# Expert tiles of 512 and of 256 slots, filled by a placement in units of 256, in place of 23 tiles of 512

## The reference

```python
gout = x @ Wgate + bgate
topv, topi = jax.lax.top_k(gout, K)              # K = 2 of E = 8
topw = jax.nn.softmax(topv, axis=-1)
...
z = (x @ W1[e] + b1[e]) * (x @ W2[e] + b2[e])     # 128 -> 256
g = z @ Wg[e] + bg[e]                             # 256 -> 256
o = g * sigmoid(g) * (z @ Wl[e] + bl[e])
y = o @ W3[e] + b3[e]                             # 256 -> 128
```

## Time and profile before

| what | value |
|---|---|
| median of 3 runs | 958.55 us (958.43 to 963.51) |
| profiled execution: span from the first to the last instruction | 882.4 us |
| median less that span: what lies around it | 76.15 us |
| PE / DVE / POOL / ACT busy, share of the span | 75% / 64% / 52% / 34% |
| mean granted TensorE clock | 0.842 of full |
| instructions | 31011 |

### The profile page before, as it was taken

The page is one execution under the profiler, slowest core; times in us unless marked ns, Lnnn a source line. Parts: engine busy times, 40 slices in busy tenths (PEclk is TensorE's granted clock), DMA queues, the critical chain, the costliest instruction groups (busy, mean ns, idle before and its releaser), DMA issues.

```text
span 882.4 us, 31011 instructions
## 1 busy us (share of the span) xinstructions
PE 658.0 (75%) x13276; PEld 502.2 (57%) x13276; DVE 568.8 (64%) x1233; ACT 299.6 (34%) x519; POOL 458.6 (52%) x519
## 2 busy tenths in 40 slices
PE   2434856877687878878898686978878788899772
PEld 2223845666465656566666555666566646676651
DVE  6888957536747865965577546864477748533573
ACT  2221024323343425342254334333433343334230
POOL 3730168634826754676475755387435662723323
PEclk9985567989887968997899898898889798999775
DMA  7221121323113214131332204131324311310350
GB/s 290 107 96 54 61 54 39 105 64 86 26 39 78 64 32 114 39 77 53 88 108 64 77 14 108 44 92 38 54 61 74 69 38 45 93 53 31 107 196 12
DMA packets 62488, 64.92 MB, mean 74 GB/s; under 512 B 39824, under 2 KB 47888, under 8 KB 62224
## 3 DMA queue, kind: packets, MB, share of 16 engines
q1 hardware_dynamic: 54880, 46.84, 17.8%
q0 software_dynamic: 5888, 12.07, 6.1%
q10 hardware_dynamic: 1584, 4.04, 1.2%
HBM read 45.35 MB, written 17.56 MB: 71 GB/s over the span
## 4 chain that ended last, share of the span: by engine, by line
PE 29%; issue 21%; POOL 20%; DVE 18%; DMA 6%; ACT 3%; SPq 3%; DVEq 0%; POOLq 0%; ACTq 0%
PE ps_shared L1629 5%; PE ps_shared L1850 4%; POOL y_d L1042 4%; POOL xs L1031 3%; PE ps_g L1625 3%; PE ps_l L1625 3%; PE ps_x L1625 3%; DVE acc L1392 3%; PE ps_shared L1767 3%; POOL sumsq L996 2%; SPq L881 2%; DMA system_d<-masked 2%; DVE solve_prod L1466 2%; PE ps_shared L1625 2%; POOL ssq_o L1068 2%
## 5 line engine op out<-in xcount | busy, mean ns | idle before, releaser
L1042 POOL DMA_INDIRECT y_d<-work,put_i x92 | 92.3, 1004 | 80.5 <-DVE work L1605 57.4
L1031 POOL DMA_INDIRECT xs<-xn_d,owner_i x92 | 94.7, 1030 | 60.2 <-issue 24.6
L1625 PE MATMUL ps_x<-xr,w_up 128*128 128x512 f32 x276 | 98.4, 476 | 17.9 <-issue 12.0
L1076 POOL TENSOR_TENSOR z<-work,z 128x512 fp32r<-128x512 f32 x46 | 60.4, 1314 | 59.5 <-ACT z L1246 59.3
L1625 PE MATMUL ps_g<-z,w_mid 128*128 128x512 f32 x276 | 83.2, 441 | 4.6 <-POOL z L1076 4.2
L1625 PE MATMUL ps_l<-z,w_mid 128*128 128x512 f32 x276 | 82.2, 436 | 1.7 <-issue 1.1
L1392 DVE SCALAR_TENSOR_TENSOR acc<-pre,late_sb,acc 128x512 f32<-128x512 f32 x72 | 59.9, 832 | 26.9 <-ACT acc L1139 25.6
L1625 PEld LDWEIGHTS ps_x<-xr,w_up 128*128 128x128 f32 x276 | 54.8, 218 | 36.5 <-issue 18.9
L1850 PE MATMUL ps_shared<-w_plain,work 128*128 128x128 f32 x368 | 58.2, 323 | 18.1 <-DVE work L1600 13.3
L1466 DVE TENSOR_TENSOR solve_prod<-solve_T,solve_L 128x1 f32<-128x1 f32 (+14 forms) x120 | 49.4, 412 | 28.7 <-DMA solve_L<-system_d 25.3
L1850 PEld LDWEIGHTS ps_shared<-w_plain,work 128*128 128x128 f32 x368 | 53.9, 232 | 22.6 <-issue 16.5
(11 more groups left out here) (252 smaller groups left out, 1420.7 us busy)
## 6 DMA issues: line engine op xcount, KB each, us to landing
w_split<-expert_split SPq DMA_DIRECT2D x23, 768.0 KB
w_plain<-expert_plain SPq DMA_DIRECT2D x23, 196.0 KB
xa_d<-xr SPq DMA_DIRECT2D x8, 512.0 KB, 2.6
xa<-xa_d SPq DMA_DIRECT2D x8, 512.0 KB, 4.0
system_d<-masked SPq DMA_DIRECT2D x8, 256.0 KB, 2.9
x_res<-hidden SPq DMA_DIRECT2D x8, 256.0 KB, 2.8
xs<-xn_d,owner_i POOLq DMA_INDIRECT x92
y_d<-work,put_i POOLq DMA_INDIRECT x92
```

The costliest lines, as they stand in the source:

```text
L1031: pool.indirect_dma_start(xs[par][:, c, :], None, xn_d.rearrange("w p (c d) -> (w p c) d", c=CPW), bass.IndirectOffsetOnAxis(owner_i[:, w ...
L1042: pool.indirect_dma_start(y_d, bass.IndirectOffsetOnAxis(put_i[:, w * CPW + c:w * CPW + c + 1], 0), y_sb[par][:, c * D:(c + 1) * D], None) ...
L1076: pool.tensor_tensor(low[:, :], up1[i], high[:, :].bitcast(FP), ALU.subtract).then_inc(S["z_low"], 1)
L1625: made = pe.matmul(to, weights[a], x[b], start=start and n == 0, stop=stop and n == 2)
```

## The change

The number of slots goes from 23 * 512 = 11776 to 16 * 512 + 7 * 256 = 9984. `UNITS = (8192 + 8 * 255) // 256 = 39` units of 256 slots, two to a big tile and one to a small one. Tiles 0 to 15 are big, tiles 16 to 22 are small. All steps of a small tile work on half the columns, with 2 gathers and 2 scatters in place of 4 and 4. Its weights are loaded and split as before. `place` now counts, for each expert, pairs of units and an odd unit, gives the pairs to big tiles and the odd ones to small tiles (pairs beyond the 16 big tiles go on into small ones), and numbers slots so that 128 neighbours share a column. `flow` gets estimates for the small tiles; `PULL` and `LEAN` stay.

```diff
-TILES = (2 * SEQS * STEPS + EXPERTS * (TILE - 1)) // TILE
-SLOTS = TILES * TILE
+UNIT = TILE // 2
+UNITS = (2 * SEQS * STEPS + EXPERTS * (UNIT - 1)) // UNIT
+BIG = 2 * SEQS * STEPS // TILE
+TILES = BIG + UNITS - 2 * BIG
-LANES = TILES * CPW
+LANES = UNITS * CPW // 2
+SLOTS = LANES * P
...
+def columns(t):
+    return CPW if t < BIG else CPW // 2
+def width(t):
+    return columns(t) * P
...
+    if name == "split" and w >= WINDOWS + BIG:
+        return [[(ACT_, 0.4)], [(DVE_, 0.45)]]
...
+    if name in FLOW_SMALL and w >= BIG:
+        return FLOW_SMALL[name]
...
+FLOW_SMALL = {
+    "load_xs": [[(POOL_, 2.6, 5.1)]],
+    "up1": [[(PE_, 0.6)], [(ACT_, 0.5)]], "up2": [[(PE_, 0.6)]], "z": [[(DVE_, 0.45)], [(ACT_, 0.45)]], "zlow": [[(POOL_, 0.75)]],
+    "mid_g": [[(PE_, 1.2)], [(ACT_, 0.5)]], "mid_l": [[(PE_, 1.2)]], "swish": [[(DVE_, 0.45)]], "times": [[(DVE_, 0.45)]],
+    "down": [[(PE_, 1.2)]], "y_out": [[(DVE_, 0.45)]], "y_put": [[(POOL_, 2.6, 5.5)]],
+}
...
-                    for c in range(CPW):
+                    for c in range(columns(w)):
+                        lane = lane_at(w) + c
                         pool.indirect_dma_start(xs[par][:, c, :], None, xn_d.rearrange("w p (c d) -> (w p c) d", c=CPW),
-                                                bass.IndirectOffsetOnAxis(owner_i[:, w * CPW + c:w * CPW + c + 1], 0)).then_inc(
+                                                bass.IndirectOffsetOnAxis(owner_i[:, lane:lane + 1], 0)).then_inc(
                                                     S[f"in_xs{par}"], 16)
...
-                    follow(dve.tensor_reduce(tiles_of[:, :], over512[:, :, :], AX.X, ALU.add))
-                    follow(dve.tensor_tensor_scan(tiles_upto[:, :], ones8[:, :], tiles_of[:, :], 0.0, ALU.mult, ALU.add))
...
+                    dve.tensor_reduce(odd_of, reached[:, :, 0], AX.X, ALU.add)
+                    follow(dve.tensor_reduce(pairs_of, reached[:, :, 1], AX.X, ALU.add))
+                    follow(dve.tensor_tensor(odd_of, odd_of, pairs_of, ALU.subtract))
+                    dve.tensor_tensor_scan(pairs_upto, ones8[:, :], pairs_of, 0.0, ALU.mult, ALU.add)
+                    follow(dve.tensor_tensor_scan(odd_upto, ones8[:, :], odd_of, 0.0, ALU.mult, ALU.add))
+                    follow(dve.tensor_scalar(all_odd[:, :], odd_upto[:, EXPERTS - 1:], EXPERTS - 0.5, None, ALU.is_gt))
...
+                    follow(dve.scalar_tensor_tensor(extra, over(pairs_of.unsqueeze(2), *by_expert), float(TILE), upto[:, :, :],
+                                                    ALU.mult, ALU.is_le))
+                    dve.scalar_tensor_tensor(extra, over(shift_of[:, :].unsqueeze(2), *by_expert), float(UNIT), extra,
+                                             ALU.mult, ALU.mult)
...
-                    for whole, of, size in ((quad_f, slot_f, CPW), (tile_f, quad_f, P)):
-                        follow(dve.tensor_scalar(whole, of[:, :, :], 1.0 / size, 0.5 / size - 0.5, ALU.mult, ALU.add))
-                        follow(dve.tensor_scalar(whole, whole, ROUND, None, ALU.add))
-                        follow(dve.tensor_scalar(whole, whole, -ROUND, None, ALU.add))
...
+                    follow(dve.tensor_scalar(column_f[:, :, :], slot_f[:, :, :], 1.0 / P, 0.5 / P - 0.5, ALU.mult, ALU.add))
+                    follow(dve.tensor_scalar(column_f[:, :, :], column_f[:, :, :], ROUND, None, ALU.add))
+                    follow(dve.tensor_scalar(column_f[:, :, :], column_f[:, :, :], -ROUND, None, ALU.add))
...
-                    product(ps_x1[:, :], [up_of(w, part, 0, i) for part in range(2)], x).then_inc(S["x1"], 1)
+                    product(ps_x1[:, 0:width(w)], [up_of(w, part, 0, i) for part in range(2)], x).then_inc(S["x1"], 1)
...
-                    for c in range(CPW):
+                    for c in range(columns(w)):
                         for k in range(FJ):
                             made = pe.matmul(ps[:, c * D:(c + 1) * D], gated[par][k][:, c * P:(c + 1) * P], down_of(w, k),
                                              start=k == 0, stop=k == FJ - 1)
```

More of the change, by code:

```diff
@@ L45, with lane_at, rows_moved @@
 FLOOR_MIN, FLOOR_MAX = 0.01, 0.1
+def columns(t):
+    return CPW if t < BIG else CPW // 2
+def width(t):
+    return columns(t) * P
+def lane_at(t):
+    return sum(columns(n) for n in range(t))
+def rows_moved(t):
+    return 16 * sum(columns(n) for n in range(t % 2, t + 1, 2))
 class Seq:
@@ new lines, in _ @@
+                    dve.tensor_scalar(units_of[:, 0:2, EXPERTS - 1], units_of[:, 0:2, EXPERTS - 1], all_odd[:, :], None, ALU.subtract)
+                    follow(dve.tensor_scalar(units_of[:, 2:4, EXPERTS - 1], units_of[:, 2:4, EXPERTS - 1], all_odd[:, :], None, ALU.add))
+                    dve.tensor_tensor(base_of[:, :], pairs_upto, pairs_of, ALU.subtract)
+                    follow(dve.tensor_scalar(last_of[:, 0], pairs_upto, 2.0, -2.0 * BIG, ALU.mult, ALU.add))
+                    follow(dve.tensor_scalar(beyond[:, :], last_of[:, 0, EXPERTS - 1:], 0.0, None, ALU.max))
@@ L1338, in _ @@
+                    follow(dve.tensor_scalar(last_of[:, 1], odd_upto, beyond[:, :], None, ALU.add))
+                    dve.tensor_tensor(past[:, :, :], over(tile_at[:, :].unsqueeze(2), P, TILES, 2 * EXPERTS),
+                                      over(last_of[:].rearrange("p q e -> p (q e)").unsqueeze(1), P, TILES, 2 * EXPERTS), ALU.is_ge)
+                    follow(dve.tensor_tensor(shift_of[:, :], last_of[:, 1], odd_of, ALU.subtract))
                     dve.tensor_reduce(row_f[:, :], past[:, :, :], AX.X, ALU.add)
+                    follow(dve.tensor_tensor(shift_of[:, :], shift_of[:, :], last_of[:, 0], ALU.subtract))
@@ L1344, in _ @@
                                                     upto[:, :, :], ALU.mult, ALU.add))
+                    follow(dve.tensor_tensor(upto[:, :, :], upto[:, :, :], extra, ALU.add))
                     for k, mine in enumerate((top1, top2)):
@@ L1357, in _ @@
                     dve.wait_ge(S["in_xn"], 16 * WINDOWS)
+                    dve.wait_ge(S["placed"], 1)
                     if w >= 2:
@@ L1648, in _ @@
                         pe.wait_ge(S["xn"], w + 1)
-                        tile = xt[w]
+                        tile, pieces = xt[w], CPW
                     else:
-                        pe.wait_ge(S[f"in_xs{par}"], 16 * CPW * loads(w - WINDOWS, 2))
-                        tile = xs[par]
-                    transposed(ps, [tile[:, c, :] for c in range(CPW)]).then_inc(S["turned"], 1)
+                        pe.wait_ge(S[f"in_xs{par}"], rows_moved(w - WINDOWS))
+                        tile, pieces = xs[par], columns(w - WINDOWS)
+                    transposed(ps, [tile[:, c, :] for c in range(pieces)]).then_inc(S["turned"], 1)
                 elif name == "beta":
@@ L1814, in _ @@
                     g = w * FJ + i
-                    x = [xr[par][:, part, :] for part in range(2)]
+                    x = [xr[par][:, part, 0:width(w)] for part in range(2)]
                     pe.wait_ge(S["x_low"], WINDOWS + w + 1)
@@ L1842, in _ @@
                     for k in range(FJ):
-                        made = product(ps_l[:, :], [gl_of(part, k, 1, i) for part in range(2)],
-                                       [part[:, :] for part in z[par][k]], start=k == 0, stop=k == FJ - 1)
+                        made = product(ps_l[:, 0:width(w)], [gl_of(part, k, 1, i) for part in range(2)],
+                                       [part[:, 0:width(w)] for part in z[par][k]], start=k == 0, stop=k == FJ - 1)
                     made.then_inc(S["l"], 1)
```

106 lines of the change are left out of this document (59 added, 47 removed).

## The result

The changed kernel takes 914.7 us (median of four) beside 958.95 us for the kernel before, run next to it: 0.9534 of its time [0.9500 to 0.9568], 44 us less. Forecast were 930.5, between 905 and 957.

What follows compares the result with a forecast made beforehand. It took a schedule bound by work queuing on four engines, with expert work in the attention's way. 882.4 - 31 + 3 = 854.4 us of span, plus 76.15 around it, gave 930.5 us against 958.55, range 905 to 957.

Steps and rivals of the forecast that it cites:

- What lies around the span "stays": Outside the profiled span: 76.15 us, the median of 958.55 less the span of 882.4, was taken to remain unchanged.
- The chain's sum of 31 us: Last common stretch, 606 to 830 us: DMAs, down, mid, z and ps_x give 35 us over 8 tiles, 31 for 7.
- 28 DMAs on POOL: Tiles 16 to 22: half the scatters and gathers on the chain, with gaps 17.4 us over 8 tiles, go.
- PE: down, mid, ps_x: Small tiles' matmuls on the chain: 6.6 us of down, 6.9 of mid and 1 of ps_x saved over 8 tiles.
- place: Routing on DVE: about ten more operations cost 3 us, between 1 and 5, all on the path.
- The clock: Rival: with less PE work the granted clock falls from 0.91 to 0.80, PE's chain grows from 61 to 69 us; 938.5; chance 0.06.
- PE's work: Tiles 16 to 22: narrower matmuls, 0.159 us each at 256 columns, save 32 us of PE at full clock.
- Half kept: Rival: the attention's dependent chain sets the pace of a window, so 15 us go and 3 come: 946.5 us; chance 0.16.
- PE's share alone: Rival: PE stays 84% busy in the last common stretch, so 42 us go and 3 come: 919.5 us; chance 0.10.
- The order at 0: All queues from the expert stage on: re-planning is worth 0, between 25 us better and 38 us worse.
- The longest wait: Sign that the prediction is wrong: POOL's or PE's longest wait grows beyond 12.7 us.
- the slower rival: Rival: a wait like 12.70 us at a queue's head in each of the last three windows costs 38 us: 968.5; chance 0.13.

Runs made afterwards that it cites:

- e11_size2: The kernel of e3_size again, in a job at the lower level (kernel before 886.39 us): 865.33 us, 0.9762 of the kernel before.
- e3_size: The changed kernel with the old planner estimates for all tiles, so small tiles in the old order, upper level: 913.2 us, 0.9502 of the kernel before.
- e13_dma2: The kernel of e5_dma in another job, at the lower level: 880.73 us beside 887.52, 0.9932 of the kernel before.
- e5_dma: e3_size with all engines' compute in small tiles back at 512 columns, so only 28 indirect DMAs are gone, upper level: 932.49 us, 0.9746 of the kernel before.
- e6_pe: e3_size with ACT, DVE and POOL back at 512 columns, so DMAs halved and only PE narrowed, upper level: 916.84 us, 0.9555 of the kernel before.
- e7_elem: e3_size with PE back at 512 columns, so DMAs halved and ACT, DVE and POOL narrowed, upper level: 929.57 us, 0.9681 of the kernel before.
- e9_scatter: e5_dma with all four gathers put back in every tile, so only 14 scatters are gone, lower level: 888.78 us, 1.0013 of the kernel before.
- e1_before: The kernel before, unchanged, run again for its trace at the upper level: 957.84 us, 0.9975 of the runs beside it, span 956.2 us.
- e2_order: The kernel before, all tiles at 512, with only the planner's new small-tile estimates, upper level: 973.5 us, 1.0124 of the kernel before.
- e10_orderp: The changed kernel with small-tile estimates for load_xs, zlow and y_put alone, a third order, lower level: 880.3 us, 0.9890 of the kernel before.
- e4_after: The changed kernel, unchanged, in another job at the upper level: 918.13 us, 0.9577 of the kernel before.
- e14_fill: e5_dma with four unused POOL operations in place of each dropped DMA, upper level: 944.8 us beside 962.39, 0.9838 of the kernel before.

## Why the prediction was right, and where it was not

The direction and the place are right, and 914.7 lies in the range, 16 us from the point. But two steps were wrong and their errors partly met, so that the point came this close is in part luck: the forecast gain of 28 us lies between the 21 us of the lower level, whose trace the sum was read from, and the 44 to 48 us of the upper, whose median it was set against.

- **What lies around the span "stays".** This step failed. Around the span lie 2 us; the 76.15 us were a span at the lower level taken against runs at the upper. A median that exceeds the profile's span by 8% should have been one of the rivals, or at least a doubt on every row. As it stands, the sum takes a saving at one level from a time at the other.
- **The chain's sum of 31 us.** It was mis-sized, to a different side at each level. Gross of place (2.6 us), the lower level gave 21 + 3 = 24 us and the upper 48 + 3, some 50 us (e11_size2, e3_size, by their ratios; both keep the old order, as the sum does). By terms:

| term | forecast, us | lower level | upper level |
| --- | --- | --- | --- |
| 28 DMAs on POOL | 15 | 9 | 27 |
| PE: down, mid, ps_x | 13 | } 15 | 18 |
| z, elementwise | 3 | } | 5 to 6, not clear of 0 |
| place | -3 | -2.6 | -2.6 |

  (Forecast terms are those of the prediction times 7/8. Measured ones are differences of ratios. The lower level's 15 us are e13_dma2 less e11_size2, two jobs of one level. The upper's first two are e5_dma and e6_pe. The third is e7_elem against e5_dma, or e3_size against e6_pe.) At the lower level the term that was too large is the DMAs', 9 us for 15: the prediction priced them by their share of the chain, and e9_scatter shows that there the scatters, the larger share, are worth 1 to 2 us as long as the gathers stay.
- **The clock.** The prediction kept 0.91 and gave its fall a chance of 0.06, on the ground that no row showed thin matmuls and the attention's small ones ran at 0.86 to 0.91. At the level of its own trace the fall came: 0.82 for 0.91 in the last stretch. The rival had 0.80 and 8 us for it, 882.4 - 31 + 3 + 8 = 862.4 us of span, and e11_size2's span is 863.9. That nearness is luck in part. Of the 7 us that are missing from the 31, 6 are missing in the DMAs' term, where the clock stood at 0.93, and PE's term with z came out at 15 for 16 in spite of the fall. What the fall cost by itself no run shows; 8 us stay an estimate. At the upper level the clock is 0.83 before and after (e1_before, e3_size), but in two steps: 0.88 with the DMAs gone, 0.83 with the matmuls narrowed. The Trainium skill ("TensorE: Matmul & The Clock Gate", "Why this matters for your kernels") has the rule that the prediction set aside: loop so that thin matmuls stay together, or pad them, else the clock goes up and down. The page's case is one in which TensorE waits for DMAs between the groups. These traces agree with it in direction, at both levels, and in e5_dma and e6_pe with one edit between them. The narrow form still won (0.9746 to 0.9555), so here half the columns weigh more than the clock.
- **PE's work.** The price of 32 us at the full clock holds: 34 us is the estimate by e5_dma and e6_pe. 256 columns took 0.147 us each where 0.159 was read off the line between the two neighbours; neither "half of 512" (0.126) nor no gain. With 0.147 the same sum gives 35.
- **Half kept; PE's share alone.** In the lower level's net gain of 21 us (forecast 28, half kept 12) the truth lies between the forecast and the half. At the upper level PE's constant share gives the better account: 168.39 us busy at 81% would be 207 us, and the stretch took 210, in an execution 9 us under its median.
- **DVE and POOL.** DVE's busy time in the stretch fell by 18.7 us (forecast 18), though by 0.27 us for each operation of 256 columns and not 0.32; the two stretches do not hold quite the same operations. POOL's fell by 26, with 22 of the 28 DMAs in that stretch.
- **place**: 2.6 us for 3, and owned's blocks gained nothing from 78 columns, as forecast (16 matmuls in 3.70 us of a period of 4.19). POOL's wait for the first w_up behind place grew with it, 17.44 to 20.58 us. The tail kept its length: 913.9 - 872.07 = 41.8 us from the last delta_T's start to the end, for 41.5.
- **The order at 0.** It is within its bounds but not zero: +11 us with full tiles (e2_order), and +15 for the third order against the old one at the lower level in one job (e10_orderp beside e11_size2). For the changed kernel itself, 0.9534 and 0.9577 beside e3_size's 0.9502 point the same way; the intervals overlap, so it isn't shown. The sign on the stretch from 124 to 606 us did not come, as far as the fifth window marks its end: its delta_T starts at 613.44 us for 616.88 in e1_before.
- **The longest wait.** The sign that POOL's or PE's longest wait grows beyond 12.7 us rested on a misreading. In the trace of before POOL already waited 14.84 us ahead of a scatter (at 652.63) and 17.44 ahead of w_up. PE's longest, behind place's mark, grew from 10.69 to 13.28 us. What the slower rival feared did come once. The wait of 12.70 (13.08 in e1_before) is gone in the new order, but the seventh window's mix_part now waits 21.48 us at the head of POOL's queue for DVE's l, until 858.94, where it waited 7.23 in e1_before. The four kernels with any of the new estimates have 21.5 to 22.9 us there (after, e4_after, e2_order, e10_orderp). All others, which keep the old order, have 6.0 to 9.8. That this wait is what the new order costs is likely and not shown.
- **What comes late next** was named rightly: ACT's wait for w_split in the last stretch grew from 7.6 us in 3 times (e1_before) to 19.3 us in 6 (e3_size), the longest 7.0.

```profile
ACT w_up L1136 <- DMA w_split<-expert_split: 19.3, 6, 7.0
```

**A version at least as good**: the small tiles with the old estimates (e3_size, e11_size2), 0.9502 and 0.9762 of the kernel before at the two levels. At the upper its lead on the changed kernel is within the intervals. At the lower it is 15 us ahead of the nearest variant of the changed kernel (e10_orderp).

**Open.** What decides the level: one chip showed both, in different jobs, and all jobs up to e7_elem and that of e14_fill had the upper. How PE's stops hang on the DMAs (their issue, their descriptors, their landing) was not tried. The changed kernel with its own full order was not run at the lower level. What the 16 us beyond POOL's time are is settled in part only. In the last stretch, 25 us shorter in e5_dma than in e1_before, PE is busy for 13 us less, its stops sum to 8.6 us for 13.2, and it is at half clock for 59 us in place of 91. Which of stops and clock drives the other isn't known. Nor is a plainer rival excluded, that a shorter and so denser stretch raises the clock by itself.

## What to carry to other kernels

Before anything is subtracted, set the profiled execution's own time against the median: a gap of some per cent can be another level of the same program, not overhead, and a saving in us does not carry from one to the other (here 21 and 48 us for one edit). Halving the columns takes nearly half of the time off matmuls (0.147 us for 0.252 here), but let the sum have the clock fall where it was high, and price it at the clock seen under narrow work. A share of the chain is no price: the scatters had the largest single one, 8.4%, and at the lower level gave hardly anything while the gathers stayed. And when step lengths in a planner's table change, run the change with the old table too: here estimates nearer to the small tiles' lengths made an order that was 15 us worse (e10_orderp).

## What the runs showed of the hardware that was not expected

- One program runs at two levels, 886 and 960 us, 8% apart on one core, steady within a job. DVE, ACT and POOL are as busy in both within 2%. PE has 6 stops of 0.3 to 0.6 us in the lower trace and 87 in the upper, and is at half clock for 279 and 380 us.
- At the upper level the stops fall on POOL's indirect DMAs: 70 of 87 in e1_before for 31% by chance, 57 of 71 in e3_size and in e5_dma for some 28%. They fall on scatters above all: 43 of 87 and 40 of 71 (e1_before, e3_size), where chance would give 14% to 15%. The gathers have 27 of 87 and 17 of 71 for 14% to 16%. At the lower level there are too few stops to say (6 in the kernel before, 5 in e11_size2, 7 in e13_dma2), with as many DMAs.
- Fewer indirect DMAs came with a higher granted clock for PE (0.83 to 0.88 in the last stretch, 0.87 with POOL filled again). Narrower matmuls lowered it (0.88 to 0.83 at the upper level, and 0.91 or 0.93 to 0.82 at the lower).
